# Source indices kept in SBUF and fewer, larger loads in a four-layer graph network kernel

## The reference

```
GAT:    e = leaky_relu(a_s[src] + a_d[dst]);  p = exp(e - segment_max(e, dst)[dst]);  z = segment_sum(p, dst)
        out = segment_sum(h[src] * (p / (z[dst] + 1e-16)), dst)
GCN:    a plain sum of table rows [src] over each node's edges, then norm and activation
HGT:    attn = sum_d(Q[dst] * K[src]) * rel_scale[edge_rel] / sqrt(16);  attn = exp(attn - max(attn))
        out = segment_sum(attn / (segment_sum(attn)[dst] + 1e-16) * V[src], dst)
SchNet: filter of each edge = MLP(edge_attr[50]) with a softplus;  out = segment_sum(h[src] * filter, dst)
```

## Time and profile before

| | us |
|---|---|
| median of 3 runs (lowest to highest) | 11721.99 (11718.76 to 11744.6) |
| profiled execution, device time | 11726.19 |
| its span, first to last instruction | 11724.5 |
| GAT edge part, 50 to 3035 | 2985 |
| GCN edge part, 3385 to 5770 | 2385 |
| HGT edge part, 5895 to 8640 | 2745 |
| SchNet edge part, 9094 to 11600 | 2506 |

### The profile page before, as it was taken

One profiled execution on the slowest core, in us unless ns is written; L12 is line 12 of the kernel. 1 busy time (PEld: TensorE's weight loads), 2 busy tenths in 40 slices (PEclk: granted clock), 3 DMA queues, 4 the chain that ended last, 5 costly groups with the idle time before them and its releaser, 6 DMA issues. The chain is left out here.

```text
span 11724.5 us, 100661 instructions
## 1 busy us (share of the span) xinstructions
PE 6639.1 (57%) x31067; PEld 5661.3 (48%) x31067; DVE 4980.5 (42%) x11243; ACT 1831.8 (16%) x3088; POOL 6141.6 (52%) x6479
## 2 busy tenths in 40 slices
PE   4555555555346666666544545455543677776674
PEld 4444444444336666666434444444432455554453
DVE  4444444444542222222355555555554344443444
ACT  0000000000110000000200000000011444444443
POOL 4455555555126666666345555555520666666662
PEclk6666666666655555555566666666655777777776
DMA  4222222222012222122133333333410222222221
GB/s 132 76 76 77 77 77 74 76 77 77 24 39 54 55 54 55 54 54 55 54 123 122 120 123 123 123 123 122 128 46 13 63 60 61 61 61 60 61 60 39
DMA packets 578005, 881.59 MB, mean 75 GB/s; under 512 B 288015, under 2 KB 382274, under 8 KB 564530
## 3 DMA queue, kind: packets, MB, share of 16 engines
q0 software_dynamic: 232704, 536.56, 16.0%
q1 hardware_dynamic: 329082, 327.61, 9.2%
q10 hardware_dynamic: 15696, 11.01, 0.3%
HBM read 842.21 MB, written 32.40 MB: 75 GB/s over the span
## 5 line engine op out<-in xcount | busy, mean ns | idle before, releaser
L623 POOL DMA_INDIRECT PM<-gat_table,TMP x1616 | 1525.4, 944 | 1487.7 <-PE ps L662 932.7
L2097 POOL DMA_INDIRECT TMP<-schnet_table,TMP x1616 | 1558.5, 964 | 1396.8 <-issue 504.0
L1603 POOL DMA_INDIRECT PM<-hgt_kv_table,TMP x1616 | 1527.5, 945 | 1340.9 <-PE ps L1635 682.8
L1157 POOL DMA_INDIRECT TMP<-gcn_table,TMP x1616 | 1527.7, 945 | 1200.1 <-issue 435.5
L1175 PE MATMUL ps<-rows,PM 16*128 16x8 f32 x3232 | 756.1, 359 | 781.3 <-DVE PM L1223 738.8
L1175 PEld LDWEIGHTS ps<-rows,PM 16*128 16x128 f32 x3232 | 717.9, 323 | 880.6 <-DVE PM L1223 767.5
L1635 PE MATMUL ps<-PM 128*128 128x136 f32 x3232 | 637.2, 366 | 734.9 <-DVE PM L1724 664.7
L1635 PEld LDWEIGHTS ps<-PM 128*128 128x128 f32 x3232 | 586.4, 264 | 771.8 <-DVE PM L1710 700.1
L460 DVE TENSOR_TENSOR AC<-AC,ps 128x128 f32 x404 | 115.7, 286 | 1795.3 <-remote 1181.6
L2124 PE MATMUL ps<-PM 128*128 128x128 f32 x3232 | 607.5, 349 | 446.7 <-issue 273.9
L1182 PE MATMUL ps<-TMP 128*128 128x128 f32 x3232 | 838.3, 441 | 26.5 <-DVE TMP L1217 16.4
(11 more groups left out here) (370 smaller groups left out, 9190.1 us busy)
## 6 DMA issues: line engine op xcount, KB each, us to landing
PM<-local_dst_row SPq DMA_DIRECT2D x101, 1024.0 KB
PM<-local_dst_row SPq DMA_DIRECT2D x202, 512.0 KB
PM<-in_attrT SPq DMA_DIRECT2D x404, 100.0 KB
PM<-gat_table,TMP POOLq DMA_INDIRECT x1616
TMP<-gcn_table,TMP POOLq DMA_INDIRECT x1616
PM<-hgt_kv_table,TMP POOLq DMA_INDIRECT x1616
TMP<-schnet_table,TMP POOLq DMA_INDIRECT x1616
TMP<-in_src_et SPq DMA_DIRECT2D x808, 2.0 KB
```

The source lines that it names most:

```text
L623: pool.indirect_dma_start(out=g[:, par, t, 0:ROW0], out_offset=None, in_=tab0_d, in_offset=bass.IndirectOffsetOnAxis(ap=idx[:, par, t:t + ...
L1157: pool.indirect_dma_start(out=g[:, b, k, :], out_offset=None, in_=tab1_d, in_offset=bass.IndirectOffsetOnAxis(ap=idx[:, b, k:k + 1], axis= ...
L1603: pool.indirect_dma_start(out=g[:, par, t, 0:2 * P], out_offset=None, in_=kv_d, in_offset=bass.IndirectOffsetOnAxis(ap=idx[:, par, t:t + 1 ...
L2097: pool.indirect_dma_start(out=g[:, b, k, :], out_offset=None, in_=tab3_d, in_offset=bass.IndirectOffsetOnAxis(ap=idx[:, b, k:k + 1], axis= ...
```

## The change

- **Indices.** `src_idx`, a tile [128, 1616], is loaded once in the start block (SP, 808 KB, ahead of the first weights; SP waits for it at the block's end). All four layers' gathers take their columns from it. The index loads of the rounds, SP's waits ahead of them and POOL's waits on them are gone.
- **Tile breaks (GAT).** One load for four rounds (26 instead of 101), with its own semaphore; DVE waits for it ahead of the carry scans.
- **Edge types (GCN).** One 128 KB load per round instead of two of 64 KB, placed in `xT`, two rounds ahead.
- **Relation rows.** ACT stores them for four rounds at a time (256 KB), HGT loads them for four rounds at a time; at HGT's start they are issued ahead of the destination rows.
- **Attributes (SchNet).** One [50, 2048] load of 400 KB per round instead of four of 100 KB, two rounds ahead, behind one wait for the round's filter products.
- `TMP` shrinks from 6470 to 5658 columns. The sizes of all buffers in it are moved accordingly.

The diff, cut to its core (what is left out does the same for the other layers):

```diff
+        src_idx = sb("src_idx", [P, T], U32)
...
+                sp.dma_start(src_idx[:, :], a["src_et"][:, 0:T]).then_inc(ld_idx, 16)
...
+                sp.wait_ge(ld_idx, 16)
...
-                def load_idx(i, par):
-                    sp.dma_start(idx[:, par, :], a["src_et"][:, bass.ds(i * ROUND, ROUND)]).then_inc(idx_ready[par], 16)
...
                     def load_breaks(i, par):
-                        sp.dma_start(tbrk[:, par, :, :], tbrk_d[:, bass.ds(i * ROUND, ROUND)].partition_broadcast(H0)).then_inc(brk_ready[par], 16)
+                        if not narrow:
+                            sp.dma_start(tbrk[:, 0, :, par * ROUND:(par + 1) * ROUND], tbrk_d[:, bass.ds(i * ROUND, ROUND)].partition_broadcast(H0)).then_inc(brk_ready[par], 16)
+                        elif i % 4 == 0:
+                            sp.dma_start(tbrk[:, i // 4 % 2, :, :], tbrk_d[:, i * ROUND:(i + 4) * ROUND].partition_broadcast(H0)).then_inc(tile_brk_ready, 16)
...
                         load_breaks(i + 1, 1 - par)
-                        for b in range(SLOTS):
-                            sp.wait_ge(g_ready[par][b], 16 * KT * (j + 1))
-                        met(sp, i)
-                        load_idx(i + 2, par)
...
-                    pool.wait_ge(idx_ready[par], 16 * (j + 1))
                     for b in range(SLOTS):
                         pool.wait_ge(agg, i * SLOTS + b + 1)
                         met(pool, i)
                         for k in range(KT):
                             t = b * KT + k
                             pool.indirect_dma_start(out=g[:, par, t, 0:ROW0], out_offset=None, in_=tab0_d,
-                                                    in_offset=bass.IndirectOffsetOnAxis(ap=idx[:, par, t:t + 1], axis=0)).then_inc(g_ready[par][b], 16)
+                                                    in_offset=bass.IndirectOffsetOnAxis(ap=src_idx[:, i * ROUND + t:i * ROUND + t + 1], axis=0)).then_inc(g_ready[par][b], 16)
                 straight(round_)
...
                         dve.wait_ge(carry_mm, 4 * i + 1)
+                        if narrow:
+                            dve.wait_ge(tile_brk_ready, 16 * (i // 4 + 1))
...
+                def load_types(i):
+                    sp.dma_start(types[:, i % 2, :], a["rel_row"][0, i * RW:(i + 1) * RW].partition_broadcast(NREL)).then_inc(ty_ready[i % 2], 16)
...
+                for i in range(NR - 2):
+                    sp.wait_ge(ty_done, (i + 1) * SLOTS)
+                    load_types(i + 2)
...
+                for q in range(RELQ):
+                    rounds_ = range(4 * q, min(4 * q + 4, NR))
+                    if q >= 2:
+                        act.wait_ge(rel_stored[q % 2], 16 * (q // 2))
+                    for i in rounds_:
+                        for b in range(SLOTS):
+                            act.wait_ge(rel_mm, i * SLOTS + b + 2)
+                            nc.scalar.copy(relw[:, q % 2, i % 4, b * KT:(b + 1) * KT, :], rel_ps[b % 2]).then_inc(rel_kept, 1)
+                    act.wait_ge(rel_kept, (rounds_[-1] + 1) * SLOTS + 2)
+                    act.dma_start(rel_d[:, rounds_[0] * ROUND * H2:(rounds_[-1] + 1) * ROUND * H2],
+                                  relw[:, q % 2, 0:len(rounds_), :, :].rearrange("p r t h -> p (r t h)")).then_inc(rel_stored[q % 2], 16)
...
+                def load_rels(q):
+                    lo, hi = 4 * q, min(4 * q + 4, NR)
+                    sp.dma_start(relw[:, q % 2, 0:hi - lo, :, :].rearrange("p r t h -> p (r t h)"),
+                                 rel_d[:, lo * ROUND * H2:hi * ROUND * H2]).then_inc(rel_ready[q % 2], 16)
...
+                        elif i % 4 == 3 and i // 4 + 2 < RELQ:
+                            sp.wait_ge(top, (i + 1) * STEPS + 2)
+                            load_rels(i // 4 + 2)
...
-                def load_attr(i, b):
-                    sp.dma_start(attr[:, b, :], a["attrT"][:, bass.ds((i * SLOTS + b) * KT * P, KT * P)]).then_inc(attr_ready[b], 16)
...
-                for i in range(NR - 1):
-                    for b in range(SLOTS):
-                        sp.wait_ge(z_mm, i * SLOTS + b + 1)
-                        met(sp, i)
-                        load_attr(i + 1, b)
-                        sp.wait_ge(gath[b], 16 * KT * (i + 1))
-                        met(sp, i)
-                        load_idx(i + 1, b)
+                def load_attr(i):
+                    sp.dma_start(attr[:, i % 2, :], a["attrT"][:, i * RW:(i + 1) * RW]).then_inc(attr_ready[i % 2], 16)
+
+                for i in range(2):
+                    load_attr(i)
+                for i in range(NR - 2):
+                    sp.wait_ge(z_mm, (i + 1) * SLOTS)
+                    load_attr(i + 2)
...
-                        pool.wait_ge(idx_ready[b], 16 * (i + 1))
                         pool.wait_ge(msg_done, i * SLOTS + b + 1)
                         met(pool, i)
                         for k in range(KT):
                             pool.indirect_dma_start(
                                 out=g[:, b, k, :], out_offset=None, in_=tab3_d,
-                                in_offset=bass.IndirectOffsetOnAxis(ap=idx[:, b, k:k + 1], axis=0)).then_inc(gath[b], 16)
+                                in_offset=bass.IndirectOffsetOnAxis(ap=src_idx[:, (i * SLOTS + b) * KT + k:(i * SLOTS + b) * KT + k + 1], axis=0)).then_inc(gath[b], 16)
 
```

More of the change, by code:

```diff
@@ L500, in build @@
         ends = A.take(2, ROUND, parts=QR)
-        tbrk = A.take(2, 2, ROUND, parts=H0)
+        tbrk = A.take(2, 2, 4 * ROUND, parts=H0)
         carry = A.take(2, 2, ROUND + 1, parts=H0)
@@ L605, in program @@
                     rounds(sp, round_, narrow)
-                for par in range(2):
-                    load_idx(par, par)
                 sp.dma_start(xn[:, :, :], a["x"].rearrange("(t p) f -> p t f", p=P)).then_inc(x_ready, 16)
@@ L1100, in build @@
         A = Arena(TMP, 0, TW)
-        idx = A.take(SLOTS, KT, dtype=U32)
         g = A.take(SLOTS, KT, P)
         oh = A.take(2, KT, P)
+        A = Arena(xT, 0, NP)
+        types = A.take(2, RW, parts=NREL, dtype=I32)
         A = Arena(PM, 0, T * H2)
-        types = A.take(SLOTS, KT * P, parts=NREL, dtype=I32)
         hp_ld, tr_ld, hp_mm, hp = sem("hgt_prep_loads"), sem("hgt_prep_type_rows"), sem("hgt_prep_type"), sem("hgt_prep_dve")
@@ L1238, in program @@
                     dve.wait_ge(ty_ready[0], 16)
-                    dve.tensor_tensor(oh16[:, 0, :], types[:, 0, :], iota_pp[0:NREL, :].to_broadcast([NREL, KT * P]), ALU.is_equal).then_inc(ty_done, 1)
+                    dve.tensor_tensor(oh16[:, 0, :], types[:, 0, 0:KT * P], iota_pp[0:NREL, :].to_broadcast([NREL, KT * P]), ALU.is_equal).then_inc(ty_done, 1)
                     prepare(0, 0)
-                    if narrow:
-                        for i in range(NR - 1):
-                            round_(i, False)
-                    else:
-                        with dve.Fori(0, NR - 1) as i:
-                            round_(i, False)
-                    round_(NR - 1, True)
+                    rounds(dve, round_, narrow)
                 def type_rows():
@@ L1506, in build @@
         layer_ends()
-        idx_ready, g_ready = sems("hgt_idx", 2), [sems(f"hgt_gathered{par}_") for par in range(2)]
+        g_ready = [sems(f"hgt_gathered{par}_") for par in range(2)]
         lr_ready, q_ready, rel_ready = sems("hgt_local_dst", 2), sems("hgt_q_rows", 2), sems("hgt_rel_rows", 2)
@@ L1585, in program @@
                     rounds(sp, round_, narrow)
-                for par in range(2):
-                    load_idx(par, par)
-                    load_rel(par, par)
+                    if not narrow:
+                        sp.wait_ge(rel_ready[1], 16 * (PAIRS + 1))
                 either(sp, program)
-                sp.wait_ge(idx_ready[1], 16 * (PAIRS + 1))
-                sp.wait_ge(rel_ready[1], 16 * (PAIRS + 1))
             @block.gpsimd
@@ L2055, in build @@
         A = Arena(PM, after_cw, T * H2)
-        attr = A.take(SLOTS, KT * P, parts=NG)
+        attr = A.take(2, RW, parts=NG)
         ex = A.take(2, 2, KT * P)
@@ L2137, in program @@
                     for b in range(SLOTS):
-                        filters_in(0, b, b)
+                        filters_in(0, 0, b, b)
                     filters_out(0, 0)
-                    if narrow:
-                        for i in range(NR - 1):
-                            round_(i, False)
-                    else:
-                        with pe.Fori(0, NR - 1) as i:
-                            round_(i, False)
-                    round_(NR - 1, True)
+                    rounds(pe, round_, narrow)
                 either(pe, program)
```

134 lines of the change are left out of this document (53 added, 81 removed).

## The result

| | before | after |
|---|---|---|
| median of 6 runs, us | 11734.44 (11718.76 to 11752.38) | 11676.68 (11672.9 to 11689.37) |
| ratio after to before | | 0.9955, 95% interval 0.9942 to 0.9969 |
| profiled execution, span | 11724.5 | 11687.6 |

A forecast was written before the change was run, and what follows sets the result against it. The prediction took each round as a loop of 16 gathers, 2.9 us delay, a DVE/ACT/PE chain and POOL's restart. Restart savings of 134 and 32 us, other parts 0, gave 11726.2 − 166 = 11,560, as a median 11,557 us; range 11,460 to 11,745.

The forecast's parts named there:

- The loop and the restart: POOL's restart in GAT, GCN and HGT: one wait instead of two saves 0.45 us at 297 stalls, 134 us.
- 0.75 - 0.30: Saving per POOL restart, taken as 0.45 us: the stalled restart shrinks to the ordinary gap between gathers.
- that results arrive only after the last gather: Edge rounds: while gathers run, results reach the waiting engine only some 2.9 us after the last gather.
- The rival that results cannot be held back by gathers: No change: POOL's restart not on the loop, the 2.9 us a coincidence of phase; time near 11,722 us, chance 0.21.
- Half of its stalls: SchNet: less regular pattern, so half of 141 stalls counted at 0.45 us each, saving 32 us.
- Tile breaks ... no row charges a steady wait to them; value 0, bounds ±41: Tile breaks, relation rows and edge types in fewer transfers: worth 0, within 41 us either way.
- The count of equal rounds: Number of restarts taken from POOL's waits, 92 + 97 + 108 = 297 in three layers, each saving 0.45 us.
- The burst of attributes: Rival, SchNet: 400 KB at once each round delays gathers, messages and POOL's restart; 11,780 us, chance 0.10.
- the stage's start: SchNet's start: the 400 KB load takes 0.7 us longer, on 2.23 us from issue to PE; stage starts together 0.

The follow-up runs named there:

- s2: Changed kernel plus a second, always satisfied wait ahead of POOL's gathers wherever the kernel before had its index wait: 11765 us, ratio to before 1.0010.
- s3: Kernel before with the index part of the change alone; all other loads as before: 11634 us, ratio to before 0.9900.
- c1: The changed kernel itself, unaltered, run again as a control: 11684.07 us beside 11747.36 for the kernel before, one run each.
- s1: Changed kernel with GAT's tile breaks loaded once per round as before: 11629 us, ratio to before 0.9896.
- p3: Changed kernel with tile breaks per round and POOL pausing behind gather 9 of 16 in each round, all layers: 10967 us, ratio to before 0.9344.
- b2: Changed kernel, tile breaks per round, POOL pauses behind gather 5 (GAT, HGT), 13 (GCN), 5 and 13 (SchNet): 10162.3 us, ratio 1.0937, chip without stalls.
- b1: Changed kernel, tile breaks per round, POOL pauses behind gather 9 (GAT), 1 and 9 (HGT, SchNet), none in GCN: 10455.9 us, ratio 1.1250, chip without stalls.

## Why the prediction was right and wrong

**The loop and the restart: right in the main.** A round is gathers, 2.9 us, chain, restart; the second wait cost 0.48 us in GAT (9.99 to 9.51), 0.40 in GCN and 0.43 in HGT, forecast 0.45. s2, which adds only the wait, has GAT's and HGT's longer stalls back. (Two slips change nothing: 0.75 - 0.30 should read 0.74 - 0.30, and 11,556 is not 11,557.) One reading was too simple: that results arrive only after the last gather. An earlier step of the same GAT round passes in the middle of the burst, 4.2 us late (PE done at 1501.94, gathers from 1494.09 to 1513.75), so results are delayed, not stopped:

```profile
1501.55 0.39 PE L683 MATMUL ps<-ones,TMP 4*64 4x1 f32 x4 [0.28 <-issue]
...
1506.16 0.15 DVE L804 COPY TMP<-ps 64x2 f32<-64x2 f32 x1 [3.47 <-remote]
```

How much of the chain passes within the burst therefore differs from round to round, and the forecast took it as fixed. The rival that results cannot be held back by gathers, for which the Trainium skill ("SBUF — State Buffer", section "SBUF: two separate sides") was quoted, fell where the stalls are: 8.7 us from PE's end to DVE's start against 0.29 on the others, and 0.58 behind a pause. That section speaks of ports; through what the results are held back is open, and so is what differs between the chips.

**SchNet: mis-sized.** Half of its stalls were counted, 32 us; it gave 58 (59 in s3, with the attribute loads as before). There, as in GCN, every batch had a second wait. s2's 102 us are more than that wait's price, as said above.

**"Tile breaks ... no row charges a steady wait to them; value 0, bounds ±41": the step that failed first.** The larger load cost 60 us in GAT (c1 against s1: 3006.2 and 2945.8). A larger load on a queue that nobody waits for shifted results that somebody waits for.

**The count of equal rounds: the step that failed second.** The sum took one stall per round, all alike, and only their restart as changed. But in GAT and HGT every 11th round had a pause and a short stall behind it, and both went with the instructions that the change removes. From round 3 on the stalls before lay 33 us (GAT) and 71 us (HGT) below as many usual ones of 9.99 and 7.86 us; the pauses themselves had cost 13 and 12 us. So 20 and 59 us of gain went.

**The sum anew,** from the two traces: restarts -47 (GAT) and -43 (HGT), all of GCN -37 and of SchNet -58 = -185. Rounds of GAT above the usual stall after the change +72, 58 of them the 23 rounds of 12.05 us. Lost short stalls less the pauses +79. Together -34 us, where the edge parts show -33. The result, 11,677 us, lies within the outer range of 11,460 to 11,745 us, but by luck of the range: it was left wide for other reasons, and the saving is a third of the forecast.

**The burst of attributes: did not decide**; SchNet became shorter, and c1 and s3 agree there to 4 us. At the stage's start it was under-priced: from SP's issue to PE's first product 5.6 us against 2.23, not 0.7 us more:

```profile
9117.91 0.71 SPq L2059 DMA_DIRECT2D PM<-in_attrT  x2
...
9123.50 2.92 PE L2084 MATMUL ps<-PM,WA 50*128 50x512 f32 x3 [11.27 <-DMA PM<-in_attrT]
```

## What to carry over

When one engine's idle time is a constant in most rounds, look at the rounds where it is not: their pattern (every 4th, every 11th) names the cause, and an average hides gains that a change may take away. Price the removal of a satisfied wait by the restart of the stalled engine, not by the wait. And ask whether a stall belongs to the kernel or to the chip that was profiled: pauses of POOL won up to 6.6% (p3) where the stalls were, and others lost 9 to 13% (b2, b1) where they were not.

## What the hardware showed that was not expected

The same kernel takes some 11,740 us on some chips and 9,290 on others, at a mean clock of 0.62 and 0.67. On the first, results of PE reach a waiting engine up to 9 us late while POOL's gathers run on end, and those that wait for their end 2.8 to 3.1 us after the last of them; on the others in 0.3 us. From DVE's start to POOL's, both released by the same sums, pass 0.74 us with two waits ahead of the gather and 0.23 with one. Where the stalls are, POOL paused 1.7 us every 11 rounds in GAT and HGT with 17 instructions a round, and not visibly with 16; in SchNet every 6.5 rounds with 20 instructions, up to 1.9 us, and 0.4 with 16.
